# Pairing two softmax chunks of a local attention, and moving the rotary addition from VectorE to GpSimd

## The reference, cut to what matters

```python
q = l2norm(q) * qs
k = l2norm(k) * ksc
q, k = rotary_xpos(q, k)          # q*cos*scale + rotate_half(q)*sin*scale
o = local_attention(q, k, v)      # window 512, causal: a query sees itself and the 512 keys before it
# inside: mask = (i < j) | (i > j + WINDOW) | (j == -1)
sim = jnp.where(mask, -jnp.finfo(sim.dtype).max, sim)
attn = jax.nn.softmax(sim, axis=-1)
out = jnp.einsum('bhwij,bhwjd->bhwid', attn, bv)
```

## Time and profile before

| | |
|---|---|
| median of 3 runs | 5190.56 us (5189.99 to 5273.63) |
| the profiled execution, its own time | 5190.56 us |
| its span (slowest core, core 1) | 5189.0 us |
| spans of the 8 cores | 5165.6 to 5189.0 us |
| DVE busy | 1983.6 us, 38% |
| ACT busy | 1718.6 us, 33% |
| POOL busy | 390.2 us, 8% |

### The profile page before, as it was taken

How to read it: one execution, slowest core, us unless ns; L and a number is a source line. 1 busy time by engine, 2 the same in 40 slices (tenths; PEclk the granted TensorE clock), 3 DMA queues, 4 the chain that set the end, 5 groups by cost and what they waited for, 6 DMA issues and landing times.

```text
span 5189.0 us, 47514 instructions; the slowest of 8 cores (5165.6 to 5189.0 us)
## 1 busy us (share of the span) xinstructions
PE 3083.0 (59%) x12400; PEld 1251.8 (24%) x12400; DVE 1983.6 (38%) x4016; ACT 1718.6 (33%) x3240; POOL 390.2 (8%) x716
## 2 busy tenths in 40 slices
PE   1476566567556445445346886975444446977952
PEld 0121122122112111212212332421221222432421
DVE  3413422431441444454454424325455455324221
ACT  3275356347436002444343101103444442102100
POOL 0000000000000003011011101112001001111100
PEclk9787777678667667555556897997555556997975
DMA  3000000000011220000001342530000000432432
GB/s 82 16 11 4 7 11 5 8 10 5 3 19 33 77 69 13 1 5 1 1 3 15 54 61 32 75 48 13 1 5 1 1 3 15 70 57 41 66 64 93
DMA packets 71817, 141.87 MB, mean 27 GB/s; under 512 B 11269, under 2 KB 23942, under 8 KB 71558
## 3 DMA queue, kind: packets, MB, share of 16 engines
q0 software_dynamic: 46080, 86.00, 11.3%
q1 hardware_dynamic: 25478, 52.82, 3.4%
HBM read 203.80 MB, written 20.97 MB: 43 GB/s over the span
## 4 chain that ended last, share of the span: by engine, by line
PE 44%; DVE 21%; ACT 15%; issue 14%; DMA 4%; DVEq 1%; ACTq 0%; POOL 0%; SPq 0%; POOLq 0%
PE SCO_A L413 13%; PE SCO_B L413 13%; PE CTX L413 12%; ACT h_sb L437 4%; DVE QK L420 4%; DMA w2b<-w_t 2%; ACT TMP L437 2%; PE PSX L413 2%; DVE negm L441 2%; DVE tmpb L431 2%; DVE tmpb L420 2%; ACT Bp L445 2%; DMA hT<-x1s 1%; DVE hT L420 1%; PE PSX L416 1%
## 5 line engine op out<-in xcount | busy, mean ns | idle before, releaser
L413 PE MATMUL CTX<-Bp,hT 128*128 128x128 bf16 x1120 | 160.0, 301 | 561.9 <-DVE Bp L447 365.5
L416 PE MATMUL PSX<-idb,Bp 128*128 128x128 bf16 x1376 | 231.3, 302 | 192.4 <-DVE Bp L426 87.3
L413 PE MATMUL SCO_A<-QK 128*128 128x512 bf16 (+1 forms) x736 | 266.5, 449 | 95.6 <-ACT TMP L437 76.2
L413 PE MATMUL CTX<-hT,w2b 128*128 128x512 bf16 x1024 | 251.0, 399 | 114.1 <-DMA w2b<-w_t 81.3
L447 POOL CAST stg<-xfT 128x513 bf16<-128x513 f32 x384 | 221.1, 624 | 1173.8 <-PE SCO_B L413 1053.3
L413 PE MATMUL SCO_B<-QK 128*128 128x512 bf16 (+1 forms) x736 | 263.5, 444 | 43.1 <-ACT h_sb L437 34.9
L437 ACT ACTIVATE h_sb<-SCO_B,negB 128x1024 bf16<-128x1024 f32 x256 | 283.9, 1109 | 0.0
L413 PE MATMUL SCO_A<-Bp,wkb 128*128 128x512 bf16 x1056 | 268.5, 390 | 19.8 <-DVE Bp L426 19.8
L437 ACT ACTIVATE TMP<-SCO_B,b1g_sb 128x512 bf16<-128x512 f32 x176 | 120.9, 687 | 479.2 <-PE SCO_B L413 479.2
L420 DVE TENSOR_TENSOR cbo<-CTX,rdb 64x512 bf16<-64x512 f32 x32 | 21.8, 683 | 662.0 <-ACT rdb L445 662.0
L413 PE MATMUL SCO_B<-Bp,wvb 128*128 128x512 bf16 x1056 | 265.9, 389 | 0.0
(11 more groups left out here) (198 smaller groups left out, 5581.8 us busy)
## 6 DMA issues: line engine op xcount, KB each, us to landing
wkb<-w1a_t POOLq DMA_DIRECT2D x88, 256.0 KB, 4.0
wvb<-w1g_t POOLq DMA_DIRECT2D x88, 256.0 KB, 4.7
w2b<-w_t POOLq DMA_DIRECT2D x64, 352.0 KB, 4.4
Bp<-x SPq DMA_DIRECT2D x16, 512.0 KB, 3.5
hT<-x SPq DMA_DIRECT2D x16, 512.0 KB, 5.5
x1s<-hT SPq DMA_DIRECT2D x16, 512.0 KB, 4.0
hT<-x1s SPq DMA_DIRECT2D x16, 512.0 KB, 4.0
out<-hT SPq DMA_DIRECT2D x16, 512.0 KB, 2.9
```

The costliest lines, as they stand in the source:

```text
L413: e.matmul(o, l, r, start=a, stop=b), reads=[lhsT, rhs], writes=[out])
L416: P.op("tensor", lambda e, o=out, i=in_, d=ident: e.transpose(o, i, d), reads=[in_, ident], writes=[out])
```

## The change

Three edits, of which the first two are in the attention stage.

The steps go in pairs: the two heads of one chunk are worked together. Each kind of operation is emitted for both before the next kind comes: both scores, both masks, then all tails that are pending (those of the pair before), both maxima, both exps, both Ln, both Exp, both `ts`. The buffers stay the same.

The two masks lie side by side in one tile Tboth. Where a chunk has five blocks, one DVE addition with a strided view covers the first and the last block (256 columns), instead of two of 128 columns.

In the rotary stage t0 to t3 are issued on POOL instead of DVE. The output of a alternates between `tmp_a` and `tmp_b`, so a2 waits for t0 and a3 for t1. The outputs of b go to four slots which hold the `rnb` tiles of chains 1, 3, 0 and 2 by number, free by then.

```diff
-        Tsame = S("Tsame", [128, 128], F32); Tprev = S("Tprev", [128, 128], F32)
+        Tboth = S("Tboth", [128, 256], F32)
+        Tprev = Tboth[:, 0:128]
+        Tsame = Tboth[:, 128:256]
...
-        def tt(out, a, b, op):
-            P.op("vector", lambda e, o=out, x=a, y=b, p=op: e.tensor_tensor(o, x, y, p),
+        def tt(out, a, b, op, eng="vector"):
+            P.op(eng, lambda e, o=out, x=a, y=b, p=op: e.tensor_tensor(o, x, y, p),
                  reads=[a, b], writes=[out])
...
-                    for ch in chains:
-                        stt(tmp_a, ch["outv"][:, slc], ch["sc"], ch["csT"][:, slc],
+                    for ci, ch in enumerate(chains):
+                        ta = (tmp_a, tmp_b)[ci % 2]
+                        tb = [rnb_slots[2][0:64, :], rnb_slots[3][0:64, :],
+                              rnb[0][0:64, :], rnb[1][0:64, :]][ci]
+                        stt(ta, ch["outv"][:, slc], ch["sc"], ch["csT"][:, slc],
                             ALU.mult, ALU.mult)
-                        stt(tmp_b, ch["bank"][0:64, :], ch["scr"], ch["snT"][:, slc],
+                        stt(tb, ch["bank"][0:64, :], ch["scr"], ch["snT"][:, slc],
                             ALU.mult, ALU.mult)
-                        tt(ch["outv"][:, slc], tmp_a, tmp_b, ALU.add)
+                        tt(ch["outv"][:, slc], ta, tb, ALU.add, eng="gpsimd")
...
+                    for g_ in grp:
+                        w1_ = min(g_["width"], 512)
+                        mm(g_["SC"][:, 0:w1_],
+                           g_["qvp"][:, g_["qc"] * 128:(g_["qc"] + 1) * 128],
+                           g_["kvp"][:, g_["base"]:g_["base"] + w1_], True, True)
+                        if g_["width"] > 512:
+                            mm(g_["SC"][:, 512:g_["width"]],
+                               g_["qvp"][:, g_["qc"] * 128:(g_["qc"] + 1) * 128],
+                               g_["kvp"][:, g_["base"] + 512:g_["base"] + g_["width"]],
+                               True, True)
+                    for g_ in grp:
+                        if g_["qc"] >= 4:
+                            scv = g_["SC"][:, 0:g_["width"]].rearrange(
+                                "p (a b) -> p a b", b=128)[:, 0::4, :]
+                            tt(scv, scv, Tboth.rearrange("p (a b) -> p a b", b=128),
+                               ALU.add)
+                        else:
+                            tt(g_["SC"][:, g_["width"] - 128:g_["width"]],
+                               g_["SC"][:, g_["width"] - 128:g_["width"]],
+                               Tsame, ALU.add)
+                    while pend:
+                        emit_tail(*pend.pop(0))
+                    for g_ in grp:
+                        red(negm[g_["z"] % 2], g_["SC"][:, 0:g_["width"]],
+                            ALU.max, negate=True)
+                    for g_ in grp:
+                        act(E_raw2[g_["z"] % 2][:, 0:g_["width"]],
+                            g_["SC"][:, 0:g_["width"]], AF.Exp,
+                            bias=negm[g_["z"] % 2], accum=den_i[g_["z"] % 2])
+                    for g_ in grp:
+                        act(negm[g_["z"] % 2], den_i[g_["z"] % 2], AF.Ln)
+                    for g_ in grp:
+                        act(rden[g_["z"] % 2], negm[g_["z"] % 2], AF.Exp, scale=-1.0)
+                    for g_ in grp:
+                        ts(En_i[g_["z"] % 2][:, 0:g_["width"]],
+                           E_raw2[g_["z"] % 2][:, 0:g_["width"]],
+                           rden[g_["z"] % 2], None, ALU.mult)
+                    for g_ in grp:
+                        pend.append((g_["i"], g_["qc"], g_["z"]))
```

More of the change, by code:

```diff
@@ L88, in host_constants @@
     c["Tprev"] = np.where(jj >= pp, 0.0, -1e30).astype(np.float32)
+    c["Tboth"] = np.ascontiguousarray(np.concatenate(
+        [c["Tprev"], c["Tsame"]], axis=1))
     c["idb"] = np.eye(128, dtype=BF)
@@ L458, in build_program @@
                        ("cq8", cq8), ("sq8", sq8), ("ckb", ckb), ("skb", skb),
-                       ("Tsame", Tsame), ("Tprev", Tprev), ("idb", idb), ("idf", idf),
+                       ("Tboth", Tboth), ("idb", idb), ("idf", idf),
                        ("ones64", ones64), ("ones128", ones128),
@@ L772, in build_program @@
                 pend = []
[L773 to L777, removed]
-                        lo = max(0, qc - 4)
[L779 to L803, removed]
@@ new lines, in build_program @@
+                zs = [(qc, i) for qc in range(NCH) for i in range(2)]
+                for z0 in range(0, len(zs), 2):
+                    grp = []
+                    for dz in range(2):
+                        z = z0 + dz
+                        qc, i = zs[z]
+                        lo = max(0, qc - 4)
+                        grp.append(dict(z=z, qc=qc, i=i, lo=lo,
+                                        nb=qc + 1 - lo, base=lo * 128,
+                                        width=(qc + 1 - lo) * 128,
+                                        SC=(SCO_A, SCO_B)[z % 2],
+                                        qvp=(QKt[0], QKt[1])[i],
+                                        kvp=(QKt[2], QKt[3])[i]))
+                    for g_ in grp:
[37 more added lines that the diff above has]
+                        pend.append((g_["i"], g_["qc"], g_["z"]))
```

## The result

The changed kernel takes 5063.2 us (median of 12 runs, 5056.4 to 5178.28). The ratio to the kernel before is 0.9748, with a 95% interval of 0.9691 to 0.9804. So the change is clear of zero, but whether it is worth more than 2% the interval leaves open. The profiled execution took 5064.65 us, 125.9 us less than the profiled execution of before. The forecast was 5071, 120 us less, in a range of 5030 to 5115.

The account below looks back on a forecast made before the run. The prediction took the kernel to be bound by latency, with no engine full. From 5190.56 us it summed - 84 (attention) - 41 (additions on POOL) - 7 (restage collision) + 12 (casts) = - 120, so 5071 us, range 5030 to 5115.

Parts of the forecast that it names:

- casts' term: Start of attention stages: restage(0) casts, now behind POOL's additions, hold up `ts` in passes 0 to 2; 12 us lost.
- attention term: Eight attention stages, each 10.5 us shorter through the paired heads; 84 us gained, bounds 76 to 92.
- serial walk: Attention pair: chain of waits from `ts` A through both heads' tails to the next exps; cycle 7.5 us against 8.07.
- thin cover: Attention pair: scores of B end some 0.3 us before the transposes of A may start; if gone, up to 0.5 us per pair.
- D: Rotary stage: how long one addition t lasts on POOL; taken as 1.2 us, with 0.56 and 1.7 as limits.
- finding POOL busy: Rotary slice: a2, after waiting for t0's slot, is also shut out by t1 until 2.15 + 2D.
- old collision: Fourth slice of passes 0 and 1, as predicted: a0 hit the restage(0) casts on POOL and lost 1.8 us.
- the part's total: Rotary stages: 41 us gained from additions on POOL plus 7 us from a0 no longer hitting restage(0).
- The 7 us within it: Rotary stages of passes 0 and 1: 4 x 1.8 us gained as restage(0) now stands behind t3.
- faster by over 2%: Whole kernel: time below the 2% border of 5087 us; chance 0.62, of which the forecast of 5040 to 5086 holds 0.6.
- same: Whole kernel: within 2%, 5087 up to 5129 us, by D nearer 1.7 or a 7.8 us cycle; rival's chance 0.3, outcome 0.34.

Follow-up runs that it names:

- pairs-only run: The changed kernel with the rotary additions t back on DVE as before; 5085.44 and 5088.48 us, ratio 0.9797 to the kernel before.
- run with two masks: The changed kernel with two mask additions of 128 columns in place of the merged one; ratio 0.9763 to the kernel before.
- four-tile run: The changed kernel with products a0 to a3 going to four tiles instead of two; 5027.61 to 5028.5 us, ratio 0.963 to the kernel before.
- one-input run: The changed kernel with products a reading PSUM in place of the SBUF cosine table (results not the reference's); 5004.18 to 5013.04 us, ratio 0.9593.
- early restage: The changed kernel with the next pass's restage(0) casts queued on POOL right behind the last projection; 5048.62 to 5052.98 us, ratio 0.9726.

## Where the prediction was right, and which steps failed

The total came out 6 us from the forecast, but by luck in part: two terms of its sum failed, on opposite sides. In the casts' term the failed step is "in passes 0 and 1 the two DMAs let the first `ts` through and the second pair's waits 1 us": a `ts` of the first pair was held in every such pass, for 4.3 to 4.5 us, and the term is + 21 us and not + 12. In the attention term the steps of the cycle were right and the gain per stage was mis-sized: 12.5 us, not 10.5, so - 100 and not - 84. PE's clock, which took some 1.5 us from each rotary stage of passes 2 and 3, was put at nothing.

**The attention pair.** The serial walk was right in its order and in nearly every step. New cycle 7.34, predicted 7.5 (7.4 to 7.6). Most of the 0.16 lies in ACT's spacing, which is 0.10 at both places where 0.10 to 0.19 was allowed for, the rest in the transposes of A, 0.79 to their copy rather than 0.84. Over 11 cycles this is 1.8 us a stage. An attention stage without casts gained 12.5 us where 10.5 was forecast: 100 instead of 84. In the pairs-only run, against before, the 11 full cycles gained 8.3 us (6.3 forecast), the four narrow ones 2.6 (1.7) and the rest of the stage 1.5 (2.5: the 7.4 us from the last even `ts` to the next projection, on which this rested, is that of the first stage; in the other seven it is 7.04).

**The merged mask.** Worth nothing, as said and as shown by the run with two masks. The thin cover named beside it, the scores of B before the transposes of A, held: these scores start at 2128.22 in the changed kernel, and the transposes at 2129.10 wait 0.20 us for `ts`, not for PE.

**The additions on POOL.** D is 1.25, predicted 1.2. b3 ends 7.06 us after a0, predicted 7.3, before 8.38. The sum was right and one sentence of it was not: I had POOL follow with t1 at once and shut DVE out, as if POOL always went first. The four-tile run shows that a DVE product already waiting gets its turn. What the prediction called finding POOL busy was the slot's wait putting a2 just behind t1's start. It gave the right number for the change and the wrong one for the four-tile run.

The rule of the Trainium skill (SBUF — State Buffer, Who interferes with whom), that whichever started first has the ports for the whole instruction, agrees with t0's 1.64, a2's 1.67 and with the one-input run, in which nothing is stretched. It names tensor_scalar in its 2-port modes among what can be held, and `ts` was held; it doesn't cover one that waits behind seven operations in turn, 4.45 us here.

**What DVE's gain brought.** By the DVE run alone a rotary stage without the old collision should have gained 3 x 1.32 + 2.1 = 6 us; passes 2 and 3 gained 4.4. The rest went to PE's clock. Before, the 16 matmuls of the fourth projection of pass 2 took 4.90 us from first to last; in the changed kernel they take 5.96 (timelines, before and changed):

```profile
2442.94 3.17 PE L413 MATMUL SCO_A<-stg,wqb 128*128 128x512 bf16 x8
2445.95 1.89 PE L413 MATMUL SCO_B<-stg,wkb 128*128 128x512 bf16 x8
```

```profile
2408.42 3.59 PE L417 MATMUL SCO_A<-stg,wqb 128*128 128x512 bf16 x8
2411.81 2.57 PE L417 MATMUL SCO_B<-stg,wkb 128*128 128x512 bf16 x8
```

The granted clock of that whole stage is 0.64 where it was 0.66, and the same 116 matmuls are busy for 43.08 us instead of 40.62. The run with the additions alone has the same rotary code behind the old attention stage: there passes 2 and 3 have a clock of 0.67 and 41.2 to 41.5 us of PE, and take 70.2 to 70.5 us, 5.9 less than before, as the sum by DVE has it. In the four-tile kernel the same stage comes at two clocks: passes 1 to 3 take 66.1 and 66.3 us where it is 0.68, and 67.8 to 68.4 where it is 0.63. The clock had not been a term of the sum. It could have: in the rows above eight matmuls of one size take 3.17 us and the next eight 1.89. Why it comes out lower behind the paired stage is not shown. The clock's loss cancelled what b3's 0.24 us beyond the forecast brought, and so the part's total, 48 us (41 + 7) forecast, 48 measured, is right partly by luck.

The 7 us within it are those of a0 and the casts. They met in the third slice of passes 0 and 1 (a0 at 2251.92; the fourth slice's is at 2268.80 and lasts 0.74), not in the fourth, as the prediction has it; the sum is the same, as every slice ends with b3.

**The casts.** That they would move into the first pairs and hold up `ts` was right, and the bound of 12 us for it too low: 21 us by the stages. The step that failed is the one on the DMAs, named above. In the first pass `ts` A was issued within the second DMA's instruction and did not get out before seven casts; in the second pass it did, and `ts` B of the same pair, which the prediction forgot, took 4.3 us. So passes 0 and 1 lost more than pass 2: first cycles of 8.0, 7.1 and 6.4 us in passes 0 to 2, 3.9 in pass 3. Against the early restage a first cycle is 3.5 to 4.2 us longer in passes 0 and 1, where 1 was forecast, and 2.6 to 2.8 in pass 2, where 4 was.

**The sum.** Forecast - 84 - 41 - 7 + 12 = - 120. By the stages it was - 100 (attention without the stall) - 48 (rotary) + 21 (stall) = - 127. The two terms that were off, 16 and 9 us, lay on opposite sides, and that is luck. Of the chances: the forecast of faster by over 2% came true in the middle value, 2.5%, and is not settled by the measurement, whose interval reaches 0.98; "same", with 0.34, is not excluded.

## What to carry to other kernels

Two strands that take turns are worth pairing, but look for what stays serial in the pair. Here the tails, emitted one strand wholly before the other, through one bank and with a cast ahead of the next exp, kept 2.0 of 7.3 us, and working them kind by kind, with the second bank and the casts moved, brought nearly twice what the change did. Work moved to an idle engine brings its queue along: see what stood behind it there, and put what has no hurry, like a cast for the next pass, where the other engine waits for PE anyway. Where two engines exclude each other, a second buffer can matter for the order of asking more than for the data.

## What the runs showed of the hardware

- A two-input addition of 64x512 f32 to bf16 takes 1.25 us on POOL and 0.68 on DVE; eight of 128x513, with one source read twice, 1.0 each on POOL.
- A product of DVE with one SBUF and one PSUM input runs at 0.74 us beside a POOL addition, which keeps its 1.26. With two SBUF inputs one of them waits.
- A DVE `ts` from bf16 to bf16 in SBUF, 128 columns, is held by POOL casts back to back, though it has one SBUF tensor input: 4.45 us in place of 0.25, and 7.6 behind eight additions of 1.0. It was held when issued 0.31 and 0.43 us before the recorded start of the first cast, too. A weight DMA's instruction on POOL with no cast behind it did not hold it: 0.25 us inside one.
- An ACT instruction that waits for nothing starts 0.10 us after the start of an accumulator read, which lasts 0.20.
- PE's granted clock was 0.63 in some and 0.68 in other stages of one kernel with the same instructions (the four-tile kernel), and the latter were 1.5 to 2.3 us shorter.
